# Attention 0 of a fused decoder kernel: next block's scores moved ahead of this block's output product, operand fetch moved, statistics one block ahead

## The chip, the cores and the metric

The kernel runs on one core of a Trainium2 chip. The metric is the device time of one execution in microseconds (us). A core has a matrix engine (TensorE, PE in the profile; its weight loads are PEld), a vector engine (VectorE, DVE), a scalar engine (ScalarE, ACT), GpSimd (POOL) and SyncE (SP, which here only issues DMAs). Each engine works through its own instructions in order; they meet at semaphores. SBUF is the on-chip memory, PSUM the banks that TensorE writes its products into.

## The reference

The input x is 32 sequences of 64 tokens with 512 features, ctx is of the same shape. Four residual stages follow each other. Only the first is touched:

```python
x = x + _L0_xattn_ref(_layernorm(x), ctx, wq, wk, wv, wo)   # 32 query heads, 8 key heads, 128 wide
x = x + _L0_ffn_ref(_layernorm(x), W0, bias0, W1, bias1)    # quantised weights and inputs
x = x + _L1_xattn_ref(_layernorm(x), ctx, ctx, ...)
x = x + _L1_ffn_ref(_layernorm(x), ...)

def _L0_xattn_ref(query, value, wq, wk, wv, wo):
    q, k, v = query @ wq, value @ wk, value @ wv            # by heads; k and v shared by 4 query heads
    scores = einsum('bhqd,bhkd->bhqk', q / sqrt(128), k)
    probs = softmax(scores, axis=-1)
    return einsum('bhqk,bhkd->bqhd', probs, v) @ wo
```

All arithmetic is float32 in the reference. The kernel splits each operand into a float16 "high" part and a float16 "low" rest and adds three products (high by high, high by low, low by high).

## The kernel before

**Preparation.** The 2048 tokens are four blocks of 512. For each block TensorE transposes 4 tiles of ctx and then 8 units of normalised x; ScalarE copies each transposed unit out of PSUM as its high part and VectorE writes the low part (units are counted by `n`, 12 to a block). The normalised x (`XN`) comes from GpSimd, which needs the mean and deviation of the block's rows (`stats_ready`). GpSimd also forms sums and differences of x, since the query product uses a scheme with seven products in place of eight. VectorE computes the statistics of block i at the head of block i: `ln_stats_vector`, called at `n % PER_BLOCK == 0` (L544), with one square root on ScalarE (L532). The finished seven operands of a block (`XT`, 1792 KB) are stored to HBM and fetched again for each later use.

**Attention 0.** Eight groups (one key head with its four query heads) by four blocks make 32 steps, called block t of group g here. Seven groups run in a hardware loop (`Fori`), the eighth is written out. In the loop body the four blocks stand unrolled. On TensorE (`group`, L805) a block is: `scores` of this block (48 small products into two PSUM banks `sc`), `queries` of the next block (seven products of 12 matrix multiplies, in the banks `pj` and `xp`), `project` (key) of the next block, `weigh_values` for the first head pair (needs the transposed probabilities `PT`), `project` (value) of the next block, `weigh_values` for the second pair (needs `OT` of the first pair out of the banks `tv`), and `project_out` (48 products of 512 columns in four tiles that alternate between the banks `xp[0]` and `xp[1]`). VectorE (L1068) does the softmax of the block first, with the additions for the next block's queries (`add_products`) between its parts, then key, output and value low parts, and last `accumulate`, which adds the four tiles of the output product to X. ScalarE has the exponentials and all high parts, GpSimd two additions and the four low query parts (`low_queries`). SyncE turns the probabilities by DMA transpose (`PT<-EH`) and then fetches the next `XT` (`load_x`, L631), which waits for the transposes.

Beside this, each group prepares a slice of the weights of the next stage: `load_weights` (DMAs on ScalarE's queue), `amax_weights`, `scale_weights`, `weights_times_rec`, `weights_to_grid`, `dequantise_weights` (GpSimd), `high_weights`, `low_weights`, transposes and stores. `PREP` says in which block a half of it runs. In block 2 the query weights of the next group are split (`high_q`, `low_q`, `high_kv`, `low_kv`). In block 0 the output weights are split (`WO`, L902 on ScalarE and L1094 on VectorE).

What the banks allow: `queries` may write `xp[0]` and `xp[1]` (its third and fourth product) only once `accumulate` of the tiles 2 and 3 of the block before has read them (`x_acc`, L732 and L735); `project_out` writes tile 2 when tile 0 is accumulated and tile 3 when tile 1 is (L799). The last group also does LayerNorm statistics and quantisation of x for the next stage on VectorE (`x_pieces`).

## Time and profile before

| what | us |
|---|---|
| three runs | 1778.66, 1781.14, 1784.40 (median 1781.14) |
| the profiled execution, its own time | 1778.68 |
| its span | 1776.9 |
| TensorE busy | 1528.1 (86%) |
| VectorE busy | 1380.6 (78%) |
| ScalarE, GpSimd busy | 847.5 (48%), 609.7 (34%) |
| mean granted TensorE clock | 0.944 |
| preparation, up to the first query product | 0 to 77.3 |
| attention 0, seven groups in the loop | 94.1 to 1009.6 |
| its last group | 1009.6 to 1133.7 |
| the three later stages | 1133.7 to 1776.9 |

In a timeline row the first number is the start in us from the start of the span, the second the length, then engine, line, operation, out<-in and the number of instructions merged; in brackets at the end is the time the engine stood idle before it and what it waited for. A busy PE row is modelled, so the step from one start to the next is the better measure of a product.

### The profile page before, as it was taken

To read this page: it belongs to the slowest core of one execution; us is meant where nothing else is said; L and a number is where in the kernel's file an instruction comes from. 1 tells how busy PE (TensorE), PEld (TensorE's weight loads), DVE (VectorE), ACT (ScalarE), POOL (GpSimd) and SP (SyncE) were. 2 spreads that over 40 slices of the span, in tenths; PEclk is the share of its full clock that TensorE was granted. 3 is DMA by queue.
4 is the path that set the end of the run, shared out by engine and by line. 5 is a ranking of instruction groups with operands and counts; after the bars stand their busy time and mean duration, and the time that the engine had idled before them with its cause. 6 is when DMAs were issued, how large, how long until landed. Compare 5 with 4: busy or idle time off the path is not lost. (4 is left out here: it accounts for less than half of the span.)

```text
span 1776.9 us, 33608 instructions
## 1 busy us (share of the span) xinstructions
PE 1528.1 (86%) x12582; PEld 947.4 (53%) x12598; DVE 1380.6 (78%) x2466; ACT 847.5 (48%) x1789; POOL 609.7 (34%) x505
## 2 busy tenths in 40 slices
PE   5698998898898898898899988779999998777686
PEld 4466565565565565565565655334454454444343
DVE  5576776676686686687677778789999996799877
ACT  3434334334334244244244333266667774688742
POOL 5435224224234233233243322101112102589720
PEclk7699999999999999999999999889999999999998
DMA  8244444344334334344353341212222242567502
GB/s 326 89 143 133 99 104 141 90 108 137 90 114 131 90 114 131 90 124 120 90 149 95 96 142 55 96 21 45 54 47 41 44 99 43 100 104 120 96 1 94
DMA packets 278895, 177.97 MB, mean 100 GB/s; under 512 B 239714, under 2 KB 256099, under 8 KB 274020
## 3 DMA queue, kind: packets, MB, share of 16 engines
q1 hardware_dynamic: 239860, 142.90, 32.0%
q10 hardware_dynamic: 38896, 33.03, 5.7%
q8 instruction: 109, 1.79, 0.4%
q14 instruction: 30, 0.25, 0.0%
HBM read 101.45 MB, written 18.87 MB: 68 GB/s over the span
## 5 line engine op out<-in xcount | busy, mean ns | idle before, releaser
L801 PE MATMUL xp<-WO,OT 128*128 128x512 f16 x1536 | 346.9, 386 | 9.5 <-DVE X L1038 9.5
L801 PEld LDWEIGHTS xp<-WO,OT 128*128 128x128 f16 x1536 | 149.0, 99 | 199.3 <-issue 32.7
L716 PE MATMUL pj<-XT,WQ 128*128 128x256 f16 x1536 | 191.3, 280 | 7.6 <-PEq L419 7.4
L891 ACT ACTIVATE E<-E 128x512 f32<-128x512 f32 x64 | 40.3, 630 | 328.0 <-DVE E L1015 327.9
L675 POOL TENSOR_TENSOR C<-C 128x512 f32<-128x512 f32 x32 | 41.2, 1288 | 397.0 <-ACT C L862 397.0
L683 POOL TENSOR_TENSOR QT<-C,QT 128x512 f16<-128x512 f32 x128 | 168.4, 1339 | 23.7 <-ACT QT L870 23.7
L1038 DVE SCALAR_TENSOR_TENSOR X<-xp,X 128x512 f32<-128x512 f32 x128 | 88.2, 690 | 110.3 <-PE xp L801 109.3
L716 PEld LDWEIGHTS pj<-XT,WQ 128*128 128x128 f16 x1536 | 152.0, 100 | 28.8 <-issue 8.1
L1244 PE MATMUL db<-W0T,XD 128*128 128x448 f16 x768 | 161.5, 362 | 0.0
L1261 PE MATMUL eb<-W1T,DT 128*128 128x512 f16 x672 | 149.4, 382 | 5.2 <-ACT EB L1336 3.4
L716 PE MATMUL xp<-XT,WQ 128*128 128x256 f16 x1152 | 136.4, 273 | 0.9
L788 PE MATMUL tv<-PT,V 64*128 64x256 f16 x768 | 59.1, 292 | 78.6 <-DMA PT<-EH 44.6
L716 PEld LDWEIGHTS xp<-XT,WQ 128*128 128x128 f16 x1152 | 111.6, 98 | 17.7 <-ACT C L862 4.8
L1244 PEld LDWEIGHTS db<-W0T,XD 128*128 128x128 f16 x768 | 76.7, 100 | 73.9 <-issue 7.1
L1261 PEld LDWEIGHTS eb<-W1T,DT 128*128 128x128 f16 x672 | 66.0, 98 | 80.0 <-issue 2.2
L870 ACT ACTIVATE QT<-C 128x512 f16<-128x512 f32 x128 | 78.5, 630 | 60.6 <-POOL C L678 43.6
L1316 ACT ACTIVATE VD<-VD,dscale 128x128 f32<-128x128 f32 x224 | 68.7, 390 | 78.5 <-DVE VD L1418 78.5
L761 PE MATMUL pj<-WKV,CT 128*128 128x128 f16 x1536 | 106.2, 237 | 0.0
L761 PEld LDWEIGHTS pj<-WKV,CT 128*128 128x128 f16 x1536 | 100.8, 108 | 8.0 <-issue 7.7
L688 POOL TENSOR_TENSOR VW<-VW,XB 128x1024 f32<-128x1024 f32 x14 | 32.9, 2351 | 209.5 <-DVE VW L115 209.5
L1493 POOL TENSOR_TENSOR VW<-VW,xscale 128x512 f32<-128x512 f32 x15 | 24.6, 1642 | 230.6 <-DVE VW L1394 221.0
L989 DVE TENSOR_TENSOR OT<-tv,OT 128x512 f16<-128x512 f32 x128 | 82.1, 683 | 26.7 <-ACT OT L883 26.0
(262 smaller groups left out, 3091.2 us busy)
## 6 DMA issues: line engine op xcount, KB each, us to landing
XT<-xt SPq DMA_DIRECT2D x31, 1792.0 KB, 7.7
W0T<-in_L_xattn_wq ACTq DMA_DIRECT2D x7, 1024.0 KB, 5.4
W0T<-in_L_xattn_wo ACTq DMA_DIRECT2D x7, 1024.0 KB, 5.2
CS<-in_ctx SPq DMA_DIRECT2D x4, 1024.0 KB, 10.2
X<-in_x SPq DMA_DIRECT2D x4, 1024.0 KB, 11.2
out<-X SPq DMA_DIRECT2D x8, 512.0 KB, 3.6
xt<-XB SPq DMA_DIRECT2D x2, 1792.0 KB, 6.2
XB<-in_L_ffn_W ACTq DMA_DIRECT2D x28, 128.0 KB, 7.0
```

The lines of the kernel that those rows point to most:

```text
L675: pool.tensor_tensor(C12[:, :], C21[:, :], C22[:, :], ALU.add).then_inc(S["q_pool"], 1)
L683: pool.tensor_tensor(q_out(1, pair, half), source[:, :], q_out(0, pair, half), ALU.subtract).then_inc(S["qt_lo"], 1)
L716: last = pe.matmul(to, WQ[:, a, w, (2 * k + m) * HEAD0:(2 * k + m + 1) * HEAD0], XT[:, b, xq, k, :].rearrange("p (b t) -> p b t", t=SEQ), ...
L761: last = pe.matmul(pj[1][:, i * P:(i + 1) * P], CT[:, a, k, own], WKV[:, b, k, 1, :], start=n == 0, stop=n == 3 * KC - 1)
L788: last = pe.matmul(tv[h][:, s * 256:(s + 1) * 256], V[rows, t % 2, a, 2 * pair + s, :], PT[rows, b, :, 2 * pair + s, :], start=n == 0, sto ...
L801: last = pe.matmul(xp[i % 2][:, :], OT[:, a, j, i * P:(i + 1) * P], WO[:, b, j, :], start=n == 0, stop=n == 3 * REP - 1)
L870: act.activation(q_out(0, pair, half), source[:, :], ACT.Copy).then_inc(S["qt_hi"], 1)
L989: dve.tensor_tensor(o_out(1, pair, h), o_bank(h), o_out(0, pair, h), ALU.subtract).then_inc(S["ot_lo"], 1)
L1038: dve.scalar_tensor_tensor(out=xt, in0=xp[i % 2][:, :], scalar=UNSCALE, in1=xt, op0=ALU.mult, op1=ALU.add).then_inc(S["x_acc"], 1)
L1244: last = pe.matmul(db[q][:, 0:NQ], XD[:, i[1] % 2, a, k, :], W0T[:, b, k, q * NQ:(q + 1) * NQ], start=False, stop=n == 3 * KC - 1)
L1261: last = pe.matmul(eb[:, :], DT[:, a, c, :], W1T[:, b, c, :], start=False, stop=c == IC - 1 and (a, b) == PASSES[-1])
L1316: last = act.activation(VD[:, r, c, :], VD[:, r, c, :], ACT.Copy, scale=ds_[:, r, c:c + 1])
```

## The change

On TensorE the scores of the next block are issued in front of `project_out` of this block, where they stood behind it, at the head of the next block. VectorE's softmax of the next block therefore runs beside this block's output product, and the four `accumulate` calls with their weight work stand between its parts. All five `add_products` run together at the head of a block. ScalarE does the softmax at the end of a block, and its `WO` part, the weight DMAs and `high_weights` change places. SyncE fetches `XT` when the queries have read it, without waiting for the transposes, and the weights' transposes stand ahead of the probabilities' transposes of the next block. GpSimd's `dequantise_weights` runs one block later, behind `low_queries`. The statistics of block i+1 in the preparation stand after the ctx units of block i. The splits of the query weights are done in two parts, with `A11` ahead of `S1`. `last_block` goes.

```diff
 # preparation (ScalarE; VectorE has the same with ln_stats_vector)
-                    if n % PER_BLOCK == 0:
-                        ln_stats_scalar(act, 0, (n // PER_BLOCK,))
+                    if n == 0:
+                        ln_stats_scalar(act, 0, (0,))
+                    if n % PER_BLOCK == BT and n // PER_BLOCK + 1 < BLOCKS:
+                        ln_stats_scalar(act, 0, (n // PER_BLOCK + 1,))
...
 # SyncE
             load_x(0, 0, 1)
+            turn_probs(0, 0)
             for g in range(GROUPS):
                 for t in range(SPG):
-                    for part, split in enumerate(("e_hi", "e_lo")):
-                        sp.wait_ge(S[split], n_of(g, t, 2, 2))
-                        sp.dma_start_transpose(...)
+                    more = g < GROUPS - 1 or t < SPG - 1
                     if g < GROUPS - 1 or t < SPG - 2:
-                        sp.wait_ge(S["pt_done"], n_of(g, t, 32, 32))
                         load_x(g, t + 1, (t + 2) % SPG)
                     for n, lo, hi in prepared(t - 1, g == GROUPS - 1):
...
+                    if more:
+                        turn_probs(g, t + 1)
...
 # GpSimd
+                    for p in prepared(t - 1, last):
+                        dequantise_weights(g, *p)
                     if t == 1 and not last:
                         sum_q(pool, g + 1)
-                    for p in prepared(t, last):
-                        dequantise_weights(g, *p)
...
 # TensorE, group(g, last)
-                    if not last or t < SPG - 1:
-                        scores(g, t)
                     if more:
                         queries(*nxt, (g, t))
                         project(*nxt, False)
...
                     weigh_values(g, t, 1)
-                    if last and t == SPG - 2:
-                        scores(g, SPG - 1)
+                    if more:
+                        scores(*nxt)
                     project_out(g, t, nxt if more else None)
...
 # ScalarE
+            def softmax(g, t, weights_of=None):
+                for jp in range(2):
+                    act.wait_ge(S["sub_done"], n_of(g, t, 2, jp + 1))
+                    act.activation(E[:, jp, :, :], E[:, jp, :, :], ACT.Exp, scale=exp_scale).then_inc(S["exp_done"], 1)
+                    if weights_of is not None:
+                        high_q(act, weights_of, ((0, 2), (2, 5))[jp])
+                if weights_of is not None:
+                    high_kv(act, weights_of)
+                for jp in range(2):
+                    act.wait_ge(S["p_done"], n_of(g, t, 2, jp + 1))
+                    act.activation(EH[:, 0, jp, :], ..., ACT.Copy).then_inc(S["e_hi"], 1)
...
 # VectorE
-            def last_block(g, t):
+            def softmax(g, t, between):
                 scores_less_max(g, t, 0)
                 scores_less_max(g, t, 1)
+                between(0)
                 sums(g, t, 0)
                 normalise(g, t, 0)
-                accumulate(g, t - 1, 0)
+                between(1)
                 sums(g, t, 1)
                 normalise(g, t, 1)
-                accumulate(g, t - 1, 1)
+                between(2)
                 low_probs(g, t, 0)
                 low_probs(g, t, 1)
...
+                between(3)
...
+                    def accumulate_and_prepare(i):
+                        accumulate(g, t, i)
+                        if i == 0:
+                            x_ahead(4)
+                        if i < 2 and t == SPG - 2 and not last:
+                            low_q(dve, g + 1, (i, i + 1))
+                        if i == 2:
+                            for p in prepared(t - 1, last):
+                                low_weights(g, *p)
+                        if t == 0 and not last:
+                            if i < 2:
+                                amax_weights(g, i)
+                            if i > 0:
+                                scale_weights(g, ((0, 3), (3, 11), (11, SCALE_STEPS))[i - 1])
+                        for p in prepared(t, last):
+                            weights_to_grid(g, *p, i)
+                    if t == SPG - 1 and not last:
+                        low_q(dve, g + 1, (2, 5))
+                        low_kv(dve, g + 1)
                     if more:
-                        add_products(*nxt, (2, 3, 4))
+                        add_products(*nxt, range(5))
...
+                    if more:
+                        softmax(*nxt, accumulate_and_prepare)
                         continue
```

Three places show where the instructions stand now. On TensorE, in the loop, at the end of block 0 (`tv` is `weigh_values`, `sc` the scores, `xp<-WO` `project_out`, `pj<-XT` the first query product), before:

```order
159 L788 MATMUL tv<-PT,V 128x256 [waits a0_ot_lo]
160 L788 MATMUL tv<-PT,V 128x256 x11
161 L801 MATMUL xp<-WO,OT 128x512 [waits a0_ot_lo,a0_kv_lo,a0_o_lo]
...
169 L801 MATMUL xp<-WO,OT 128x512 x11
170 L767 REGISTER_ALU [waits a0_kv_lo]
171 L771 MATMUL sc<-KT,QT 128x64 [waits a0_qt_lo]
172 L771 MATMUL sc<-KT,QT 128x64 x47
173 L724 REGISTER_ALU
174 L716 MATMUL pj<-XT,WQ 128x4x64 [waits a0_q_lo,a0_xt_ld]
```

The scores follow the output product, and the next queries follow the scores. The same place on TensorE with the change:

```order
157 L799 MATMUL tv<-PT,V 128x256 [waits a0_ot_lo]
158 L799 MATMUL tv<-PT,V 128x256 x11
159 L778 REGISTER_ALU [waits a0_kv_lo]
160 L782 MATMUL sc<-KT,QT 128x64 [waits a0_qt_lo]
161 L782 MATMUL sc<-KT,QT 128x64 x47
162 L812 MATMUL xp<-WO,OT 128x512 [waits a0_ot_lo,a0_kv_lo,a0_o_lo]
...
171 L812 MATMUL xp<-WO,OT 128x512 x11
172 L735 REGISTER_ALU
173 L727 MATMUL pj<-XT,WQ 128x4x64 [waits a0_q_lo,a0_xt_ld]
```

The scores, now of the next block, stand ahead of the output product, and the queries of the block after it follow the output product at once. On VectorE, from block 2 into block 3 (`X<-xp` is `accumulate`, `WQ` `low_q`, `ST` and `E` the softmax, `EH` `low_probs`, `C<-pj` the first of `add_products`), with the change:

```order
248 L1052 SCALAR_TENSOR_TENSOR X<-xp,X 128x512 [waits a0_xp_done]
249 L1021 SCALAR_TENSOR_TENSOR XB<-VW,XB 128x1024 [waits a0_wt_hi]
250 L113 TENSOR_SCALAR XB<-XB 128x1024 [waits a0_wbits]
251 L1046 TENSOR_TENSOR EH<-E,EH 128x512 [waits a0_e_hi] x2
253 L1052 SCALAR_TENSOR_TENSOR X<-xp,X 128x512 [waits a0_xp_done]
254 L115 TENSOR_TENSOR VW<-VW,XB 128x1024 [waits a0_wm_done]
...
256 L328 SCALAR_TENSOR_TENSOR WQ<-W0T,WQ 128x512 [waits a0_q_hi]
258 L328 SCALAR_TENSOR_TENSOR WQ<-S4F,WQ 128x512 [waits a0_q_hi]
260 L328 SCALAR_TENSOR_TENSOR WQ<-W0T,WQ 128x512 [waits a0_q_hi]
262 L333 SCALAR_TENSOR_TENSOR WKV<-W0T,WKV 128x1024 [waits a0_kvw_hi]
```

Tile 3 (row 253) is accumulated behind the whole softmax of the next block and the weight work, and three splits of the query weights come after it; before, all five splits stood behind tile 0. On ScalarE, in block 0 (`QT` is `high_queries`, `WO` the output weights, `KT` and `V` key and value, `OT` the attention output), with the change:

```order
59 L880 ACTIVATE QT<-C 128x512 [waits a0_q_sum]
60 L919 REGISTER_ALU
61 L921 ACTIVATE WO<-W0T 128x2048 [waits a0_xp_done,a0_so_ld]
62 L883 REGISTER_ALU
63 L884 ACTIVATE KT<-xp 128x512 [waits a0_kv_done]
64 L891 REGISTER_ALU
65 L893 ACTIVATE OT<-tv 128x2x4x64 [waits a0_pv_done]
66 L893 ACTIVATE OT<-tv 128x2x4x64
67 L888 ACTIVATE V<-pj 128x512 [waits a0_kv_done]
```

The same place on ScalarE before, where `WO` stands in front of the four query parts:

```order
54 L896 ACTIVATE EH<-E 128x512 [waits a0_p_done]
55 L900 REGISTER_ALU
56 L902 ACTIVATE WO<-W0T 128x2048 [waits a0_xp_done,a0_so_ld]
57 L867 REGISTER_ALU
58 L870 ACTIVATE QT<-C 128x512 [waits a0_q_pool]
59 L869 ISA
60 L870 ACTIVATE QT<-C 128x512 [waits a0_q_sum]
```

`WO` has moved from ahead of the four `QT` copies to behind them, directly in front of the key.

## Rows read from the trace of the kernel before

**Rows 1.** Waits of TensorE, whole run: total us, times, longest.

```profile
PE tv L788 <- DMA PT<-EH: 44.6, 28, 2.2
PE tv L788 <- DVE OT L989: 34.0, 24, 6.8
PE xp L801 <- DVE X L1038: 9.5, 10, 1.6
```

**Rows 2.** Waits of GpSimd in the preparation, 0 to 77 us.

```profile
POOL XN L475 <- DVE nmr L182: 26.7, 4, 12.2
```

**Rows 3.** Timeline, second block of the preparation.

```profile
24.66 2.46 DVE L159 BATCH_NORM_STATS2 bn<-X 128x6 f32<-128x512 f32 x4
...
29.14 1.52 POOL L475 TENSOR_SCALAR XN<-X,rstd,nmr 128x512 f32<-128x512 f32 x2 [6.46 <-DVE nmr L182]
...
33.63 1.51 POOL L475 TENSOR_SCALAR XN<-X,rstd,nmr 128x512 f32<-128x512 f32 x2
```

**Rows 4.** Timeline of GpSimd and VectorE, last group, statistics beside GpSimd.

```profile
1091.20 1.26 POOL L249 TENSOR_TENSOR VW<-VW 128x512 f32<-128x512 f32 x1 [2.08 <-DVE VW L115]
...
1091.25 1.24 DVE L175 TENSOR_TENSOR ln_work<-guess 128x4 f32<-128x4 f32 x1
```

**Rows 5.** Timeline of TensorE, one block of a group in the loop.

```profile
387.99 1.56 PE L771 MATMUL sc<-KT,QT 128*128 128x64 f16 x48
389.39 2.79 PE L716 MATMUL pj<-XT,WQ 128*128 128x256 f16 x24
...
398.56 2.75 PE L755 MATMUL xp<-CT,WKV 128*128 128x512 f16 x12
402.58 0.83 PE L788 MATMUL tv<-PT,V 64*128 64x256 f16 x12 [1.27 <-DMA PT<-EH]
...
407.04 0.83 PE L788 MATMUL tv<-PT,V 64*128 64x256 f16 x12 [0.84 <-DVE OT L989]
407.80 10.54 PE L801 MATMUL xp<-WO,OT 128*128 128x512 f16 x48
418.17 1.56 PE L771 MATMUL sc<-KT,QT 128*128 128x64 f16 x48
```

**Rows 6.** Timeline of TensorE around a loop jump.

```profile
343.01 10.53 PE L801 MATMUL xp<-WO,OT 128*128 128x512 f16 x48
...
358.12 1.85 PE L771 MATMUL sc<-KT,QT 128*128 128x64 f16 x40 [2.63 <-issue]
...
370.08 2.75 PE L755 MATMUL xp<-CT,WKV 128*128 128x512 f16 x12
```

**Rows 7.** Timeline of VectorE, softmax and weight work in the loop.

```profile
371.25 2.92 DVE L1094 SCALAR_TENSOR_TENSOR WO<-W0T,WO 128x2048 f16<-128x2048 f32 x1
...
395.26 1.65 DVE L1027 TENSOR_TENSOR E<-E,ST 128x512 f32<-128x512 f32 x1
...
397.43 2.35 DVE L1032 TENSOR_TENSOR EH<-E,EH 128x512 f16<-128x512 f32 x2
...
444.15 2.95 DVE L326 SCALAR_TENSOR_TENSOR WQ<-W0T,WQ 128x1024 f16<-128x1024 f32 x3
```

**Rows 8.** Timeline of VectorE, softmax of the last block, GpSimd idle.

```profile
1106.99 0.69 DVE L1027 TENSOR_TENSOR E<-E,ST 128x512 f32<-128x512 f32 x1
...
1110.36 1.28 DVE L1032 TENSOR_TENSOR EH<-E,EH 128x512 f16<-128x512 f32 x2
```

**Rows 9.** Timeline of ScalarE, block 0 of a group.

```profile
366.73 1.90 ACT L902 ACTIVATE WO<-W0T 128x2048 f16<-128x2048 f32 x1
```

**Rows 10.** DMA issues by line, 345 to 500 us: count, median us to landing.

```profile
PT<-EH SPq DMA_TRANSPOSE x10, 2.7
```

**Rows 11.** Landing of the weight slices' DMAs (line L656).

```profile
DMA to landing us min/median/max: 2.5/5.0/8.4
```

**Rows 12.** Timeline of TensorE, last group.

```profile
1059.28 1.46 PE L788 MATMUL tv<-PT,V 64*128 64x256 f16 x12 [3.37 <-DVE OT L989]
...
1097.68 1.46 PE L788 MATMUL tv<-PT,V 64*128 64x256 f16 x12 [6.78 <-DVE OT L989]
```

More of the change, by code:

```diff
@@ L321, in high_kv, with low_q @@
             act.activation(WKV[:, 0, :, :, :], SKV[:, :, :, :], ACT.Copy, scale=WEIGHT_SCALE).then_inc(W["kvw_hi"], 1)
-        def low_q(dve, g):
-            for n, (first, size, source, sign) in enumerate(Q_SPLITS):
+        def low_q(dve, g, part=(0, 5)):
+            for n in range(*part):
+                first, size, source, sign = Q_SPLITS[n]
                 dve.wait_ge(W["q_hi"], g * 5 + (n + 1))
@@ L827, in _ @@
             project(0, 0, True)
+            scores(0, 0)
             with pe.Fori(0, GROUPS - 1) as g:
@@ L888, in group @@
                     more = not (last and t == SPG - 1)
-                    for jp in range(2):
-                        act.wait_ge(S["sub_done"], n_of(g, t, 2, jp + 1))
-                        act.activation(E[:, jp, :, :], E[:, jp, :, :], ACT.Exp, scale=exp_scale).then_inc(S["exp_done"], 1)
-                        if more and jp == 0:
-                            copy_lone(*nxt, 0)
-                    for jp in range(2):
-                        act.wait_ge(S["p_done"], n_of(g, t, 2, jp + 1))
-                        act.activation(EH[:, 0, jp, :], E[:, jp, :, :].rearrange("p b k -> p (b k)"), ACT.Copy).then_inc(S["e_hi"], 1)
-                        if more and jp == 0:
-                            copy_lone(*nxt, 1)
+                    if more:
+                        copy_lone(*nxt, 0)
+                        copy_lone(*nxt, 1)
+                    for p in prepared(t, last):
+                        weights_times_rec(g, *p)
+                    if more:
+                        high_queries(*nxt)
                     if t == 0:
@@ L902, in group @@
                         act.activation(WO[:, 0, :, :], SO[:, :, :], ACT.Copy, scale=WEIGHT_SCALE).then_inc(S["o_hi"], 1)
-                    if more:
-                        high_queries(*nxt)
-                    for p in prepared(t, last):
-                        weights_times_rec(g, *p)
                     if last and t in (1, 2):
                         stats_x(act, t - 1)
-                    for p in prepared(t - 1, last):
-                        high_weights(g, *p)
-                    if t == 0 and not last:
-                        load_weights(act, g)
                     if more:
@@ L928, in group @@
                         load_o(act, g + 1)
+                    if more:
+                        softmax(*nxt, g + 1 if t == SPG - 2 and not last else None)
                     if t == SPG - 1 and not last:
@@ L948, in _ @@
             act.wait_ge(xt_st[3], 16)
+            softmax(0, 0)
             with act.Fori(0, GROUPS - 1) as g:
@@ L1076, in x_ahead @@
                             x_pieces[n](dve, t - 1)
-                    if last and t == SPG - 1:
-                        last_block(g, t)
-                        continue
-                    scores_less_max(g, t, 0)
-                    scores_less_max(g, t, 1)
-                    for jp in range(2):
-                        sums(g, t, jp)
-                        normalise(g, t, jp)
-                        if more:
-                            add_products(*nxt, (jp,))
-                    low_probs(g, t, 0)
-                    low_probs(g, t, 1)
+                    def accumulate_and_prepare(i):
[5 more added lines that the diff above has]
+                        if i == 2:
+                            for p in prepared(t - 1, last):
+                                low_weights(g, *p)
[4 more added lines that the diff above has]
+                                scale_weights(g, ((0, 3), (3, 11), (11, SCALE_STEPS))[i - 1])
+                        for p in prepared(t, last):
+                            weights_to_grid(g, *p, i)
+                    if t == SPG - 1 and not last:
+                        low_q(dve, g + 1, (2, 5))
+                        low_kv(dve, g + 1)
                     if more:
-                        add_products(*nxt, (2, 3, 4))
+                        add_products(*nxt, range(5))
                     if t == 0:
@@ L1099, in group @@
                     x_ahead(1)
-                    for p in prepared(t - 1, last):
-                        low_weights(g, *p)
                     if more:
@@ L1109, in group @@
                     x_ahead(3)
-                    if last and t == SPG - 2:
+                    if more:
+                        softmax(*nxt, accumulate_and_prepare)
                         continue
-                    for i in range(BT):
-                        accumulate(g, t, i)
-                        if i == 0:
-                            if t == SPG - 2 and not last:
-                                low_q(dve, g + 1)
-                            x_ahead(4)
-                        if t == 0 and not last:
-                            if i < 2:
-                                amax_weights(g, i)
-                            if i > 0:
-                                scale_weights(g, ((0, 3), (3, 11), (11, SCALE_STEPS))[i - 1])
-                        for p in prepared(t, last):
-                            weights_to_grid(g, *p, i)
-                        if i == 1 and t == SPG - 2 and not last:
-                            low_kv(dve, g + 1)
+                    dve.wait_ge(S["x_acc"], n_of(g, t, 4, 2))
+                    for n in range(3):
+                        x_pieces[n](dve, t - 1)
+                    accumulate(g, t, 0)
+                    x_pieces[3](dve, t - 1)
+                    accumulate(g, t, 1)
+                    x_pieces[4](dve, t - 1)
+                    accumulate(g, t, 2)
+                    accumulate(g, t, 3)
             add_products(0, 0, range(5))
@@ L1130, in _ @@
             low_value(0, 0)
+            softmax(0, 0, lambda n: None)
             with dve.Fori(0, GROUPS - 1) as g:
```

42 lines of the change are left out of this document (17 added, 25 removed).

## The prediction

> **What bounds the kernel now.** I read the page first: TensorE is busy for 86% of the span, VectorE for 78%, so the changed part, 0 to 1134 us, is worth what TensorE waits there. The waits of TensorE say where [rows 1]: 44.6 us in 28 waits for the turned probabilities `PT`, 34.0 us for the low part of `OT` from VectorE, 9.5 us for `accumulate` to free an `xp` bank. Then the timeline of one block in the loop [rows 5]. From start to start the scores take 389.39 - 387.99 = 1.40 us, the seven query products 398.56 - 389.39 = 9.17 (1.31 each), the output product 418.17 - 407.80 = 10.37. From the key product's start to the second `weigh_values` it is 8.48 us, of which 1.27 and 0.84 are waits, so 6.4 of work. The reader is to see why `PT` is late: between the scores' end and its use lie only the queries and the key product, 12 us, while the softmax, the additions threaded into it and the transposes need more. The waits of the preparation [rows 2, 3] show another bound: GpSimd stood 26.7 us waiting for statistics, 12.2 of it for the first block, which stays, and 14.5 for blocks 1 to 3. Last comes the loop jump [rows 6]: from the end of the output product (353.54) to the key product (370.08) 16.5 us pass, where 10.6 us of scores and queries stand, so a jump costs about 6 us. It stays; it now falls on the queries.
>
> **Preparation.** What moves are three sets of statistics, one block ahead; no instruction is added. Statistics take 29.14 - 24.66 = 4.5 us on VectorE, and a half block on GpSimd 33.63 - 29.14 = 4.5 us [rows 3]. Bound above: the 14.5 us of waiting, since then GpSimd runs through. Against it: the small operations now stand beside a busy GpSimd. In the last group such a 128x4 operation took 1.24 us from just after GpSimd's start to just before its end [rows 4], where it takes about 0.2 us alone. Block 0 also has its statistics pushed in front of its own low parts. If about half of the seven small operations wait 0.7 us each, statistics take 7 us; placing the blocks one after another, GpSimd then waits 0.9 us before the fifth half block and 2.7 before the seventh. I take 14.5 - 3.6 = 11 us gained, bounds 0 and 14.5. (The Trainium skill, SBUF — State Buffer, "Who interferes with whom", says that the VectorE operation that comes second blocks until GpSimd's has finished. The row agrees for one operation. If all seven waited, an estimate, statistics would take 9 to 10 us and the gain would be gone; that is a rival below.)
>
> **The loop: what goes.** The scores of the next block now lie 10.37 + 9.17 + 2.6 us ahead of the use of `PT`: 22 us of cover. The chain needs about 16.2 us on VectorE (below) and 2.7 for the transposes [rows 10], or about 22 in block 2, where the weights' transposes stand ahead of them on SyncE; there the queries are late too, so it holds. All 44.6 us go. The `OT` waits came because VectorE reached the low parts late, behind softmax and additions. Now it does the five additions as the products end and is idle when the key arrives; what stays is the last group, 3.37 + 6.78 [rows 12], where the statistics for the next stage stand in front as before. 23.8 us go. The 9.5 us for `xp` go in this form and return in another. Together 44.6 + 23.8 + 9.5 = 77.9 us. `XT` is fetched at the queries' end instead of after the transposes, 18 us ahead of its use; it waited nowhere worth a row, so I cost that at nothing, and its cover is that 18 us. The moved weight DMAs and `dequantise_weights` hide in the same way, with the weight landing as the exception named below.
>
> **The loop: what comes.**
> First, `WO` in block 0. ScalarE now does it behind the last query part, which ends 1.4 us after the queries; 1.90 us [rows 9] bring it to 3.3, VectorE's part of 2.92 [rows 7] to 6.3, the low key and two low `OT` parts (0.65 each) to 8.3 or, if a GpSimd operation is in front, 8.7. The second `weigh_values` would start at 6.4. So 2.1 us in each of eight groups: 17 us. Bounds 0 and 3.
>
> Second, the fourth query product, which waits for tile 3's `accumulate`, now behind the whole softmax. Count from the start of the scores, T = 0. TensorE: output product to T = 11.8, third product at 14.4 (needs tile 2), fourth at 15.7 (needs tile 3). VectorE is free of `OT` at T = 2.0. A 512-column operation fills 0.6 to 0.7 us, the two `low_probs` 1.28 with GpSimd idle [rows 8], where they took 2.35, and the normalising 1.65 in place of 0.69, beside GpSimd [rows 7]. I take the short ones, since `low_queries` has ended before T = 0. Block 2: maximum and subtraction 2.7 (T = 4.7); tile 0, a 1024-column split and one grid step 2.35 (7.0); sum, reciprocal, normalise 1.55 (8.6); tile 1, split and grid 2.35 (10.9); 1.55 (12.5); tile 2, low weights and grid 2.4 (14.9); `low_probs` (16.2); tile 3 (16.8); last grid step 1.15 (18.0); and the third split, which the fourth product also needs, 0.6 (18.6). That is 18.7 - 15.7 = 3.0 us late, seven times: 21 us. The splits' price is from 2.95 for two wide and one narrow [rows 7]. Block 0, with the two maxima of the weights and fifteen small scale steps instead: tile 3 at 16.3, 0.6 us late, seven times: 4 us. Block 1: 14.3; block 3: 14.0, in time. Tile 1 is due at 9.2 for the output product's last tile; block 2 has it at 9.2, block 0 at 8.6, without room to spare.
>
> Third, the last group. In blocks 1 and 2 the maxima of x (2.4 us) now stand ahead of the softmax and fifteen scale steps (3 us) between tiles 0 and 1: the output product waits 1.1 and 2.6 us, twice: 7.4. The last block has no queries to cover the softmax: `PT` lands at T = 19.2, the output product ends at 15.5: 3.7 us. Together 11 us, bounds 4 and 18.
>
> The sum: 11 + 77.9 - 17 - 21 - 4 - 11 = 36 us less. The profiled execution took 1778.68, so 1743; it lies 2.5 us under the median of the three runs. I forecast that median less the same 36: 1745 us. The granted clock I leave out of the sum: 62 waits of 1.4 us on average [rows 1] become some 20 of 2 us.
>
> **Rivals.**
> 1. The preparation gains nothing: GpSimd's operations hold up every small statistics operation. For it: the row of 1.24; against it: a GpSimd that has to wait for the statistics holds nothing up, so the delay ends itself. 1745 + 11 = 1756.
> 2. VectorE becomes the bound, and the kernel slower. Place: tile 3 in front of the fourth product. Mechanism: the softmax pays the contended price. Normalising 0.96 us more, twice, and `low_probs` 1.07 more are 3.0 us in each block. Tile 3 then comes at 19.3, 17.3, 21.6 (with split) and 17.0 against 15.7: 3.6 + 1.6 + 6.0 + 1.3 = 12.5 us a group instead of 3.6; seven times 8.9 is 62 us more: 1807. It decides from about 5 us a group more than I count (36 / 7), 1.7 us a block. For it: the long prices stood in the loop before [rows 7]; against it: GpSimd ends its queries 2 to 3 us ahead of the scores.
> 3. The weight slices land late in block 0. They are issued 0.7 and 1.5 us after T = 0; the first maximum wants them at T = 5.3. Landing was 2.5 to 8.4 [rows 11], the long ones beside `XT`, which has landed by now. At 8.4 the maximum starts at 9.9 and tile 1 and tile 3 come 4.6 later: 4.6 us a group, 32 us: 1777, no change that counts.
> 4. The new waits don't show, since VectorE and ScalarE run ahead further than I place them: 17 + 25 us back, and the preparation at its bound: 1745 - 45 = 1700.
>
> **How the numbers follow.** About 0.3% (5.3 us) is what can be told from no change. Forecast with its neighbours, 1725 to 1762: 0.50. Rival 1, and smaller gains up to 1775: 0.20 (the skill's rule, all seven waiting, is 0.12 of it). Rival 4 and between, below 1725: 0.12. Rival 3 and like ones, 1776 to 1786: 0.06. Rival 2, slower: 0.12. So faster 0.82, same 0.06, slower 0.12. The range from 1712 to 1774 leaves out half of rival 4, rival 3 and rival 2.
>
> **What would show it.** In the profile after, TensorE's waits for `PT` fall under 8 us. GpSimd's waits for statistics fall from 26.7 to about 16, and the first query product starts at 66 in place of 77.3. In each group a wait of about 2 us stands before the second `weigh_values` of block 0, on `OT`, and one of about 3 us before the fourth query product of block 2's end, on `WQ`. The normalising falls to 0.7 us in the median. A wait before the fourth product in all four blocks, or an `accumulate` that holds the output product's last tile in the loop, would be rival 2; a first query product still at 77 us rival 1. The forecast is wrong if TensorE waits more than 12 us a group beside the jump.

## The result and the profile after

| | before | after | predicted |
|---|---|---|---|
| median of the runs, us | 1779.90 (1777.11 to 1784.40) | 1691.51 (1689.94 to 1694.35) | 1745 (1712 to 1774) |
| profiled execution, own time | 1778.68 | 1689.94 | 1743 |
| ratio | | 0.9503 (95% interval 0.9478 to 0.9528) | |

Faster, as forecast, but by 88 us and not by 36: outside the range, and beyond rival 4 (1700). The gain by place, from the two profiled executions:

| stretch | before | after | difference | predicted |
|---|---|---|---|---|
| up to the first query product | 77.30 | 67.65 | -9.65 | -11 |
| from there to the first query of the loop | 18.59 | 18.33 | -0.3 | 0 |
| seven passes of the loop | 915.07 | 834.12 | -80.95 | -30 |
| last group, from its queries on | 122.76 | 125.16 | +2.4 | +5 |
| the three later stages | 643.18 | 642.94 | -0.2 | 0 |

(The predicted 30 is 70.2 us of waits that the loop holds, less 15 for `WO`, 21 and 4 for the fourth product; the last group has the rest of the sum.) The error stands in one row. The table of busy times by stretch tells more of it; its columns are stretch, length, then busy us and instructions of PE, PEld, DVE, ACT and POOL, then the granted clock, the DMA share and GB/s. The loop before and the later stages before:

```profile
95.89:1010.96 915.07, 821.26 (x7393) 554.66 (x7394) 667.44 (x995) 352.02 (x630) 322.45 (x224) 0.96 0.41 114
1133.72:1776.90 643.18, 543.61 (x3959) 281.90 (x3974) 555.78 (x1134) 416.72 (x1023) 213.22 (x197) 0.95 0.35 69
```

The same of the kernel after:

```profile
85.98:920.10 834.12, 797.54 (x7393) 537.23 (x7393) 610.31 (x1005) 353.25 (x628) 305.88 (x224) 0.99 0.43 123
1045.26:1688.20 642.94, 543.70 (x3959) 281.94 (x3974) 556.09 (x1134) 417.49 (x1023) 213.53 (x197) 0.95 0.35 69
```

TensorE does the same 7393 matmuls in the loop with 23.7 us less busy time, at a granted clock of 0.99 in place of 0.96, and stands idle for 57.2 us less (93.8 before, 36.6 after). What it waited for before, in the loop alone (total us, times, longest; "issue" is idle time in which it waited for no semaphore that the profile shows):

```profile
PE tv L788 <- DMA PT<-EH: 41.6, 24, 2.2
PE sc L771 <- issue: 22.6, 12, 2.6
PE tv L788 <- DVE OT L989: 21.8, 21, 2.4
PE xp L801 <- DVE X L1038: 6.8, 7, 1.0
```

And after, which answers to [rows 1]:

```profile
PE xp L727 <- DVE WQ L328: 16.8, 7, 2.4
PE tv L799 <- DVE OT L1003: 10.0, 7, 1.5
PE pj L727 <- ACT C L872: 8.5, 7, 2.1
PE xp L727 <- DVE X L1052: 0.5, 2, 0.3
```

The three rows of before that the prediction named are gone. In their place stand the two waits that it named, on `WQ` and `OT`, and one that it did not, on `C`. But the row "issue", 22.6 us, is gone too, and the prediction had said that it stays.

The timeline of TensorE around a loop jump after, which answers to [rows 6]:

```profile
196.04 10.52 PE L812 MATMUL xp<-WO,OT 128*128 128x512 f16 x48
206.40 2.78 PE L727 MATMUL pj<-XT,WQ 128*128 128x256 f16 x24
209.02 2.78 PE L727 MATMUL xp<-XT,WQ 128*128 128x256 f16 x24
213.12 1.49 PE L727 MATMUL pj<-XT,WQ 128*128 128x256 f16 x12 [1.32 <-ACT C L872]
```

The queries start 10.36 us after the output product, at full speed: the jump between them costs nothing. The next thing to be seen is a wait on `C`, since ScalarE comes late to empty the first product. Its timeline there (ACTq is its queue of DMA issues):

```profile
210.47 0.67 ACTq L675 DMA_DIRECT2D w0t<-XB  x1
211.31 0.60 ACTq L677 DMA_DIRECT2D w1t<-W0T  x1
212.47 0.60 ACT L872 ACTIVATE C<-pj 128x512 f32<-128x512 f32 x1 [8.13 <-PE xp L727]
```

The first product could have been emptied from about 209. ScalarE stood at `store_weights`, behind the softmax, until the weights' transposes had landed.

The wait on `WQ` on TensorE, and VectorE ahead of it:

```profile
180.71 2.31 PE L727 MATMUL xp<-XT,WQ 128*128 128x256 f16 x12 [2.40 <-DVE WQ L328]
182.82 2.35 PE L727 MATMUL pj<-XT,WQ 128*128 128x256 f16 x12
185.01 1.47 PE L727 MATMUL xp<-XT,WQ 128*128 128x256 f16 x12
```

```profile
178.24 0.69 DVE L1052 SCALAR_TENSOR_TENSOR X<-xp,X 128x512 f32<-128x512 f32 x1
178.84 1.22 DVE L115 TENSOR_TENSOR VW<-VW,XB 128x1024 f32<-128x1024 f32 x1
179.97 0.69 DVE L328 SCALAR_TENSOR_TENSOR WQ<-W0T,WQ 128x512 f16<-128x512 f32 x1
```

This is the predicted chain: tile 3, last grid step, third split. Its wait is 2.4 where 3.0 were worked out, but the two products behind it take 2.31 and 2.35 in place of 1.47. The busy table of the four microseconds ahead of the wait and of the stretch behind it shows the granted clock (third number from the end) at 1.00, the upper of its two levels (2.4 GHz), and then at 0.57, mostly the lower (1.2 GHz):

```profile
174.22:178.31 4.09, 4.09 (x37) 3.43 (x35) 4.09 (x7) 1.23 (x2) 0.00 (x0) 1.00 0.16 37
180.71:184.00 3.29, 3.29 (x18) 2.39 (x19) 3.26 (x5) 0.00 (x0) 0.32 (x1) 0.57 0.96 67
```

VectorE's softmax runs at the short prices in the loop (normalising and low probabilities; count, busy us, mean ns), against the long ones of [rows 7]:

```profile
L1041 DVE TENSOR_TENSOR E<-E,ST 128x512 f32<-128x512 f32 x62 | 42.9, 692 | 2.1
L1046 DVE TENSOR_TENSOR EH<-E,EH 128x512 f16<-128x512 f32 x62 | 40.0, 685 | 0.1
```

In the preparation GpSimd's wait for statistics, after [rows 2]:

```profile
POOL XN L477 <- DVE nmr L182: 15.6, 3, 12.0
```

And waits of the two kinds worked out for the last group:

```profile
976.22 2.75 PE L812 MATMUL xp<-WO,OT 128*128 128x512 f16 x12 [1.03 <-DVE X L1052]
981.47 2.75 PE L812 MATMUL xp<-WO,OT 128*128 128x512 f16 x12 [2.50 <-DVE X L1052]
...
1026.27 0.83 PE L799 MATMUL tv<-PT,V 64*128 64x256 f16 x12 [1.91 <-DMA PT<-EH]
```

### The profile page after: what moved, and what is told of

It reads as the page before. It is cut to its first block and busy times, and to the rows that moved or that the text cites. A ratio compares the mean times of both kernels' runs of the same rounds, so it can differ in the third digit from the quotient of the medians.

```text
span 1688.2 us, 33559 instructions
## 1 busy us (share of the span) xinstructions
PE 1496.0 (89%) x12582; PEld 926.8 (55%) x12598; DVE 1316.3 (78%) x2466; ACT 845.8 (50%) x1783; POOL 592.4 (35%) x505
## 5 line engine op out<-in xcount | busy, mean ns | idle before, releaser
L812 PE MATMUL xp<-WO,OT 128*128 128x512 f16 x1536 | 342.7, 382 | 7.4 <-DVE X L1052 7.4
L812 PEld LDWEIGHTS xp<-WO,OT 128*128 128x128 f16 x1536 | 148.2, 98 | 187.0 <-issue 18.3
L727 PEld LDWEIGHTS pj<-XT,WQ 128*128 128x128 f16 x1536 | 153.5, 101 | 47.6 <-ACT C L872 10.5
L694 POOL TENSOR_TENSOR QT<-C,QT 128x512 f16<-128x512 f32 x128 | 161.1, 1291 | 23.7 <-ACT QT L880 23.7
L727 PE MATMUL xp<-XT,WQ 128*128 128x256 f16 x1152 | 142.7, 277 | 17.8 <-DVE WQ L328 16.8
L880 ACT ACTIVATE QT<-C 128x512 f16<-128x512 f32 x128 | 73.6, 623 | 107.8 <-POOL C L689 95.6
L1265 PEld LDWEIGHTS eb<-W1T,DT 128*128 128x128 f16 x672 | 66.1, 99 | 79.9 <-issue 2.3
L905 ACT ACTIVATE EH<-E 128x512 f16<-128x512 f32 x64 | 40.3, 630 | 123.2 <-DVE E L1041 123.2
L1003 DVE TENSOR_TENSOR OT<-tv,OT 128x512 f16<-128x512 f32 x128 | 82.4, 686 | 18.2 <-ACT OT L893 15.1
L987 DVE SCALAR_TENSOR_TENSOR C<-pj,C 128x512 f32<-128x512 f32 x64 | 44.3, 692 | 62.7 <-ACT C L872 32.4
L772 PE MATMUL pj<-WKV,CT 128*128 128x128 f16 x1536 | 91.3, 219 | 0.0
L772 PEld LDWEIGHTS pj<-WKV,CT 128*128 128x128 f16 x1536 | 85.9, 98 | 6.8 <-issue 6.5
L766 PE MATMUL xp<-CT,WKV 128*128 128x512 f16 x384 | 88.1, 379 | 0.0
```

Of the source, the lines that this page charges most:

```text
L694: pool.tensor_tensor(q_out(1, pair, half), source[:, :], q_out(0, pair, half), ALU.subtract).then_inc(S["qt_lo"], 1)
L727: last = pe.matmul(to, WQ[:, a, w, (2 * k + m) * HEAD0:(2 * k + m + 1) * HEAD0], XT[:, b, xq, k, :].rearrange("p (b t) -> p b t", t=SEQ), ...
L766: last = pe.matmul(xp[1][:, :], WKV[:, a, k, 0, :], CT[:, b, k, tokens], start=n == 0, stop=n == 3 * KC - 1)
L772: last = pe.matmul(pj[1][:, i * P:(i + 1) * P], CT[:, a, k, own], WKV[:, b, k, 1, :], start=n == 0, stop=n == 3 * KC - 1)
L812: last = pe.matmul(xp[i % 2][:, :], OT[:, a, j, i * P:(i + 1) * P], WO[:, b, j, :], start=n == 0, stop=n == 3 * REP - 1)
L880: act.activation(q_out(0, pair, half), source[:, :], ACT.Copy).then_inc(S["qt_hi"], 1)
```

## The experiments

Medians are compared with the runs of before on the same chip: 1780.1 for the first four, 1780.0 for the next four, 1782.3 for the last three.

**The two parts alone.** `e1_stats_only` is before with the statistics moved; `e2_loop_only` is after with them moved back:

```diff
-                    if n % PER_BLOCK == 0:
-                        ln_stats_vector(dve, 0, (n // PER_BLOCK,), x_ld)
+                    if n == 0:
+                        ln_stats_vector(dve, 0, (0,), x_ld)
+                    if n % PER_BLOCK == BT and n // PER_BLOCK + 1 < BLOCKS:
+                        ln_stats_vector(dve, 0, (n // PER_BLOCK + 1,), x_ld)
```

> The kernel before with the preparation's part of the change alone (statistics one block ahead). Theory: the parts are separate, and the first query product comes 9.7 us earlier, as in the changed kernel: about 1770 us, the loop unchanged. Rival: the loop's first fetches or the weights' landing swallow it and the time stays at 1778 to 1781.

> The changed kernel with the preparation put back as it was. Theory: the loop alone is worth 79 us: 1701 us, first query product at 77. Rival: the parts help each other (the preparation's early end starts the fetches of the first group earlier), and the sum of the two kernels' gains is more than 3 us off 88.

Measured: 1769.2 (0.9943, 0.992 to 0.9967), first query product at 67.9; and 1699.3 (0.9552, 0.952 to 0.9583), at 76.3. The gains are 10.9 and 80.8, together 91.7 against 88.4. The 3.3 us between lie inside the intervals (4 to 6 us to either side). So far as these can tell, the parts are separate, and the missing 52 us are the loop's.

**The place of the jump's target.** The loop's code differs little, but its first instruction stands 97 places later in the changed kernel: the scores of the first block, `scores(0, 0)`, now stand once ahead of the loop (peeled off), 48 matmuls of two instructions and a wait. Section 3 of the page counts the fetches of code (packets, MB, share). Before:

```profile
q8 instruction: 109, 1.79, 0.4%
```

After, six fewer, as many as there are jumps back:

```profile
q8 instruction: 103, 1.69, 0.4%
```

```diff
+                for _ in range(194):
+                    pe.wait_ge(ident_ready, 2)
```

> The kernel before with 97 wait instructions, already satisfied, added on TensorE at the end of the preparation, where TensorE waits 7.4 us anyway. They do nothing but move the loop's first instruction 97 places on, to where it stands in the changed kernel within the blocks of 256 instructions in which code is fetched (one fetch moves 16 KB; before has 11 fetches in one pass of the loop, the changed kernel 10). Theory: the jump's cost hangs on that place. The second issue wait of each jump (2.4 to 2.6 us, after eight matmuls) goes, and with it the slower queries behind it: 22.6 us of issue waits fall to 8 or less, and 6 jumps by 3.5 to 6 us are 21 to 36 us: 1743 to 1759. Rival: a jump costs the same wherever it lands, and it was the reordering of the work that hid it: 1779 as before, issue waits still 22.

> The changed kernel with 159 such wait instructions: its loop's first instruction then stands where it stood in the kernel before (97 + 159 = 256). Theory: the stall at the jump returns, now on the first query product: 2.5 us and slower queries, 6 times, 15 to 21 us (up to 36 if the first issue wait returns too), and up to 3 us of the waits themselves in the preparation: 1707 to 1730. Rival: the order of work hides the jump wherever it lands: 1692 to 1695.

Measured: 1758.3 (0.9901, 0.9863 to 0.9938) and 1707.9 (0.96, 0.9566 to 0.9635). Before with 97 has 103 fetches; its issue waits in the loop, and the timeline around a jump:

```profile
PE sc L773 <- issue: 4.6, 6, 1.5
```

```profile
339.63 10.53 PE L803 MATMUL xp<-WO,OT 128*128 128x512 f16 x48
351.70 1.57 PE L773 MATMUL sc<-KT,QT 128*128 128x64 f16 x48 [1.54 <-issue]
353.11 1.15 PE L718 MATMUL pj<-XT,WQ 128*128 128x256 f16 x9
```

The 48 scores are one run now, and the second wait is gone; issue waits in the loop fall by 18.0 us. The loop takes 889.26, 25.8 less than before, since TensorE's busy time falls too, by 15.1 (821.26 to 806.21), and the waits for `PT` and `OT` take 7.1 of that back. After with 159 has 109 fetches; the same two views:

```profile
PE pj L729 <- issue: 13.8, 8, 2.5
```

```profile
337.25 1.04 PE L729 MATMUL pj<-XT,WQ 128*128 128x256 f16 x8
340.79 2.40 PE L729 MATMUL pj<-XT,WQ 128*128 128x256 f16 x16 [2.50 <-issue]
```

Eight matmuls, then 2.50 us of nothing: the picture of [rows 6] on another product. So the stall belongs to the place at which a jump lands, and the rival is refuted in both directions. A mere shift in time does not do it: `e1_stats_only` starts its loop 9.6 us earlier and keeps 109 fetches and 19.5 us of issue waits, and `e2_loop_only` starts 8.9 us later than the changed kernel and keeps 103 and 0.2. The reading that fits is that with a few instructions left in a fetched block the engine runs out before the next one has come; stalls and fetches were counted, not matched one by one.

Two sizes were off, and that 1707.9 lies in the range told is luck. The added waits themselves moved the first query product of the second kernel by 10.5 us (to 78.14) and that of the first by 2.7, where up to 3 were told. And the loop of the second is only 5.8 us longer though its issue waits are 13.8, since the wait on `C` falls from 8.5 to 2.0 and TensorE's busy time by 1.7: one wait covered another. In the changed kernel, then, this stall would cost 5.8 us of the loop, where its absence is worth 25.8 to the kernel before.

**The clock behind the waits.** `e10_before_warm` is before with

```diff
                         project(*nxt, False)
+                    for _ in range(6 if more and t >= 2 else 0):
+                        pe.matmul(tv[0][:, :], WKV[:, 0, 0, 0, :], CT[:, 0, 0, 0:BLOCK], start=True, stop=True)
                     weigh_values(g, t, 0)
```

> The kernel before with six idle matmuls of 512 columns (1.3 us) added on TensorE between the key product and weigh_values in blocks 2 and 3 of each group, where it waits 2.2 us for the turned probabilities; their result is overwritten. Nothing is waited for less. Theory: the slow matmuls behind these waits (the value product 240 ns on average a matmul, where it is 219 in the changed kernel) are the granted clock falling in an idle stretch; with work in it the clock stays, and of the 23.7 us by which TensorE's busy time in the loop differs between the two kernels 10 to 18 come back: 1762 to 1770 us, waits for PT some 1.3 us shorter each. Rival: the clock follows from the share of work over a longer time or from the jump, and idle matmuls in the wait change nothing: 1778 to 1782.

Measured 1770.8 (0.993, 0.9906 to 0.9953), 11.5 us less by the medians, just short of the theory's 1762 to 1770. The value product in the loop (matmuls, busy us, mean ns), before and with the idle matmuls:

```profile
L761 PE MATMUL pj<-WKV,CT 128*128 128x128 f16 x1344 | 94.8, 240 | 0.0
```

```profile
L761 PE MATMUL pj<-WKV,CT 128*128 128x128 f16 x1344 | 79.9, 219 | 0.0
```

One value product behind such a wait before, with the busy times and the granted clock (0.61) of that stretch, and the same one with the idle matmuls:

```profile
337.84 4.48 PE L761 MATMUL pj<-WKV,CT 128*128 128x128 f16 x48
337.84:342.25 4.41, 4.41 (x50) 4.30 (x48) 2.92 (x4) 1.30 (x3) 2.15 (x2) 0.61 1.00 312
```

```profile
337.20 2.85 PE L761 MATMUL pj<-WKV,CT 128*128 128x128 f16 x48
```

The granted clock is 1.00 in the second (337.20 to 340.19). 79.9 is the value products' time in the changed kernel too. The slow ones, 14.9 us, are the price of TensorE standing up to 2.2 us ahead of them; the waits for `OT` took 6.9 of it back (21.8 to 28.7). The loop is 8.9 us shorter (906.13); its issue waits are 4.3 less (18.3), which nothing here explains. In the changed kernel the waits for `PT` are gone, and the 14.9 with them.

**The new waits, one at a time.** `WO` put back ahead of the query parts on ScalarE:

```diff
+                    if t == 0:
+                        ... # WO's three lines
                     for p in prepared(t, last):
                         weights_times_rec(g, *p)
                     if more:
                         high_queries(*nxt)
-                    if t == 0:
-                        ... # WO's three lines
```

> The changed kernel with ScalarE's part of WO put back ahead of the query parts (where it stood before the change). Theory: the wait of 1.43 us before the second weigh_values of block 0 (eight times, 11.5 us) is the price of WO behind the queries, as the prediction's first term has it; ScalarE has 3.06 us idle just ahead of the first query part, so nothing else gets late: 1680 us. Rival: the wait is VectorE's, behind GpSimd's operations, and WO is not its cause: 1691.

Measured 1672.3, 19 us under the changed kernel where 11 were expected. The 10.0 us of `OT` waits are gone from the loop and 1.5 from the last group; 8.7 us more came from TensorE's busy time (797.54 to 788.89): behind the same wait of 2.40 on `WQ` in the same pass the granted clock of the next products is 1.00 in place of 0.57:

```profile
179.79:183.73 3.94, 3.94 (x37) 3.53 (x37) 3.90 (x6) 0.00 (x0) 0.98 (x1) 1.00 0.81 56
```

But it is not one kernel against the other. The fourth product has this wait in each of seven passes; at full speed it takes 1.48. In the changed kernel it is slow in six (1.71 to 2.62) and not in one, with `WO` in front it is slow in one alone. The fast one of the changed kernel, and the slow one with `WO` in front (11 of its 12 matmuls):

```profile
777.15 1.48 PE L727 MATMUL xp<-XT,WQ 128*128 128x256 f16 x12 [2.40 <-DVE WQ L328]
```

```profile
527.78 2.53 PE L727 MATMUL xp<-XT,WQ 128*128 128x256 f16 x11 [2.40 <-DVE WQ L328]
```

The granted clock behind them is 1.00 and 0.54. So the same wait is followed by either level in either kernel. Why, and by which way `WO`'s place won these 8.7 us, the runs do not tell.

VectorE's order ahead of a new group (block 2):

```diff
+                            if i < 3:
+                                accumulate(g, t, i)
+                                low_q(dve, g + 1, (i, i + 1))
...
+                            elif i == 2:
+                                accumulate(g, t, 3)
+                            else:
+                                low_q(dve, g + 1, (3, 5))
+                                low_weights(g, 0, *PREP[0][1:])
+                                weights_to_grid(g, 1, *PREP[1][1:], 2)
+                                weights_to_grid(g, 1, *PREP[1][1:], 3)
```

> The changed kernel with VectorE's order changed in the block ahead of a new group alone: the third weight split and the accumulate of tile 3 come ahead of the low probabilities, the low weights and the last two grid steps behind them. Theory: the wait of 2.4 us before the fourth query product (seven times, 16.8 us) goes, and with it the two slow query products behind it (2.3 instead of 1.47 each, 12 us more): 1663 us, granted clock in the loop 1.00. Rival: VectorE does the same work in the same time, so the wait comes back at the sixth or seventh product or before weigh_values: 1680 or more.

Measured 1676.8, 15 us less: between the two theories. The wait on `WQ` and the slow products went (busy time 787.91), and this came up in its place:

```profile
PE pj L727 <- DVE C L987: 10.8, 7, 1.5
```

The last query product waits 1.5 us for the first addition, which now stands behind the weights' steps. The rival had that right, for 10.8 of 28 us.

The stores of the turned weights issued by SyncE:

```diff
                     if more:
                         turn_probs(g, t + 1)
+                    if t == SPG - 1 and g < GROUPS - 1:
+                        store_weights(sp, g)
```

> The changed kernel with the two stores of the turned weights issued by SyncE, behind the transposes of the probabilities, instead of ScalarE. Theory: ScalarE stands at these stores until the weights' transposes land, 3.3 us past the end of the first query product that it has to empty, and that is the wait for C (8.5 us in 7): 1683 us. Rival: in SyncE's queue the stores hold up the operands of the next block or the next transposes, and waits for XT or PT come up instead: 1692 or more.

Measured 1680.7, 11 us less. The wait on `C` falls from 8.5 to 1.9, which is the first pass alone, ahead of any store; nothing came up for `XT` or `PT` in the loop. The loop is 12.2 us shorter (821.92), and 6.0 of that is TensorE's busy time (797.54 to 791.50): behind the wait on `WQ`, still 2.40, the fourth product is slow in two passes of seven.

All three edits together, and then the last two grid steps divided around the additions, with the maxima and scales of x one place later in the last group:

```diff
                     if t == SPG - 1 and not last:
+                        add_products(*nxt, (0, 1))
                         low_kv(dve, g + 1)
+                        add_products(*nxt, (2, 3, 4))
+                        weights_to_grid(g, 1, *PREP[1][1:], 3)
...
                         if i == 0:
-                            x_ahead(4)
+                            x_ahead(3)
+                        if i == 3:
+                            x_ahead(4)
```

> The three edits together on the changed kernel. Theory: they stand in different places and add up: 11.5 + 28 + 8.5 = 48 us: 1643 us, seven passes of the loop in 790 us (778 of it work). Rival: the waits hide one another, and the sum falls short by 10 us or more: 1653 or above.

> The three edits of before, with the last two grid steps of the weights split: one stays ahead, the other and the low halves of the key and value weights move between and behind the five additions of the first queries of a new group; and in the last group the maxima and scales of the next stage's input each stand one place later (maxima behind tile 0's accumulate, scales behind tile 3's). Theory: the wait of 1.5 us that came up before the last query product (10.8 us in 7) was VectorE's additions behind those steps, and goes; in the last group the waits for X of 7.4 us go and those for OT fall from 9.1 to about 6: 1659 - 11 - 9 = 1639 us. Rival: VectorE's work stays the same and only moves the wait, now to the key product or to weigh_values: 1650 or more.

Measured 1659.1 (0.9317, 0.9281 to 0.9352) and 1647.1 (0.9237, 0.922 to 0.9253). The first falls 16 us short of its sum, as its rival had it: 10.8 of it is the wait of 1.5 us above, 2.1 the wait on `C` of the first pass, and the three later stages, which no edit touches, took 645.67 in place of 642.94. Nor do the gains of the single runs add up (19, 15 and 11): TensorE's busy time in the loop fell by 8.7, 9.6 and 6.0 in them and by 11.1 with all three, so the slow products behind `WQ` are won only once. The second is the fastest kernel here, 44 us under the changed one, and ends between its theory and its rival: the 10.8 went, 2.3 came up at the key product (`WKV`) and 2.9 at the jump; the last group takes 118.47 in place of 123.57.

**The early fetch of the operands.** After, with `load_x` behind `turn_probs` on SyncE:

```diff
-                    if g < GROUPS - 1 or t < SPG - 2:
-                        load_x(g, t + 1, (t + 2) % SPG)
...
                     if more:
                         turn_probs(g, t + 1)
+                    if g < GROUPS - 1 or t < SPG - 2:
+                        load_x(g, t + 1, (t + 2) % SPG)
```

> The changed kernel with the operands of the next block fetched behind the transposes of the probabilities on SyncE, in the order of the kernel before, instead of directly behind the queries. Theory: the transposes are issued 16 to 18 us after the scores, now that those are a block ahead, and the operands land some 8 us behind that, 13 to 15 us past the time at which the queries want them, in each of 30 blocks: 2080 to 2200 us; the early fetch is what lets the scores stand ahead at all. Rival: the fetch has cover enough and its place is worth nothing: 1690 to 1700.

One run: 2087.7. The largest wait of TensorE:

```profile
PE pj L727 <- DMA XT<-xt: 362.8, 31, 15.9
```

That is 11.7 us a block, where 13 to 15 were expected. The prediction cost this edit at nothing, with 18 us of cover; that was right, and it is at the same time the condition of the whole gain.

## Why the prediction was wrong in size, step by step

**Preparation: right.** GpSimd's wait for statistics was told as 12.2, 0.9 and 2.7; it is 15.6 in three waits, of 12.0, 0.5 and 3.1, at the places named. 11.1 us are won there, 9.65 arrive at the first query product, at 67.65 where 66 was told, and `e1_stats_only` has 10.9 by the medians. Rival 1 is out.

**What goes in the loop: right.** All 70.2 us of waits for `PT`, `OT` and X.

**What comes in the loop: 40 predicted, 36 measured; near in sum, partly by luck.** `WO`: 2.1 a group predicted, 1.43 measured, cause shown by putting it back. Fourth product of a new group: 3.0 predicted, 2.4 measured, cause shown by changing VectorE's order. Fourth product in block 0: 4 us predicted, 0.5 measured. Not foreseen: 8.5 us on `C`, 6.6 of it since `store_weights` stands ahead of `copy_lone` on ScalarE and waits for the weights' transposes. The prediction has no term for that: of the weights' DMAs it says that they "hide in the same way", without looking for the wait in front of a DMA's issue. Without these 8.5 us the new waits are 27, not 40.

**The last group: right in kind, its sizes partly by luck.** X was told at 7.4 and is 7.4, but only 5.5 of it stand in the two blocks named (1.03, 2.50 and 1.98); 1.9 are in the last block's own output product, where before had 1.8. `PT` was told at 3.7 in the last block and is 1.9 there, with 0.9 one block earlier. Of what was counted as going, 2.0 on `OT` in the last block stayed as well. The stretch is 2.4 us longer, where about 5 were told.

**Rival 2 is out:** VectorE's normalising ran at 0.69 throughout (0.691 to 0.693 in all 64). Where it was looked at, GpSimd had ended (163.4) before the softmax began (164.3).

**The step that failed** is "a jump costs about 6 us. It stays; it now falls on the queries". It went: 22.6 us of issue waits fell to 0.2. [rows 6] show the larger part of it, 2.63 us, and the row just ahead of that one shows that eight matmuls had run:

```profile
355.09 0.40 PE L771 MATMUL sc<-KT,QT 128*128 128x64 f16 x8 [1.54 <-issue]
```

A cost that comes after eight matmuls is no fixed price of a jump. The peeled scores moved the target 97 places on, away from the end of its block by the reading above. Padding alone gave 18 us of the issue waits and 25.8 us of the loop back to the kernel before, and padding alone brought the stall back in the changed one. The predicted 6 us hold more than the waits: from the end of the output product to the key product the six jumps of before take 95.2 us, where 10.57 each of work stand, so 31.8 us too many (5.3 a jump), 22.6 of them waits and 9.2 slower products behind the stall. With the padding it is 4.6 us, all of it waits.

**The term left out** is the clock: "62 waits of 1.4 us become some 20 of 2 us" was read as no change. TensorE's busy time fell by 23.7 us, 14.9 of it the value products behind the waits for `PT`, and the idle matmuls show the cause of those; the 9.2 behind the stall are in it too. By the rows of the loop, 22.4 us of issue waits and these 23.7 are 46 of the 52 us that were missed; the rest is small terms that came out lower. That is a count of rows, and no run takes both terms out together: as the second padded kernel shows, with the stall in place part of the wait on `C` would have gone. Rival 4 came nearest in time, but its reason, new waits that do not show, was not what happened: they show at 36 us.

Open: the first of the two issue waits of a jump, 0.8 to 1.7 us in before, is 0.77 on average in the padded one (4.6 in 6), gone in the changed one but for 0.2 at one jump, and 0.3 to 0.7 in `e9_best`; the padding does not explain it, and no run separates it.

## What to carry to other kernels

A stall at a loop's jump has to be read for what precedes it: if a few instructions run and then nothing, as here after eight matmuls, suspect the place of the target, and move it by idle instructions ahead of the loop to find out; here this changed the price of every jump. Ask also which waits cover one another: the place alone was worth 25.8 us of the loop in one kernel and 5.8 in the other. A wait of 2 us on TensorE can cost more than its 2 us, so price the products behind it at both speeds that the trace shows and carry that as a term. Before a term is put at nothing because a DMA hides it, look for what the issuing engine waits for, and what stands behind it there.

## What was not expected of the hardware

The stall after eight matmuls (2.4 to 2.6 us before, 1.7 to 2.5 in the padded changed kernel) followed the place of the code in both kernels, with 109 fetches where it stood and 103 where it did not. The granted clock behind one and the same wait of 2.40 us differed from pass to pass: 0.53 to 0.67 in six passes of the changed kernel and 1.00 in one, and with `WO` in front slow (0.54) in one of seven. And a wait that is already satisfied is not free: in the two padded kernels TensorE's sequencer stood 10.7 and 17.7 us at the end of the preparation, 0.11 us for each of the 97 and 159 instructions (7.4 and 7.6 without them).
